# Gated delta attention and an expert layer: attention steps written out, zero-state products left out, balanced assignment on shares

## What is computed

```python
# attention, per head (8 heads, 128 x 128 state), token by token
Sst = Sst * a_t
kv = k_t @ Sst
delta = (v_t - kv) * b_t
Sst = Sst + outer(k_t, delta)          # Sst = 0 at the start of each sequence
o_t = q_t @ Sst * scale
# o -> rms_norm, gate, @ Wo; then x + h; then relu(m @ W_fc)^2 @ W_proj
# experts: assignment balanced by 20 Sinkhorn rounds on la = -logits / 0.05
for _ in range(20):
    la = la - logsumexp(la, axis=-1)   # over the 8 experts
    la = la - logsumexp(la, axis=-2)   # over the 4096 tokens
pi = exp(la)                           # top 2 of pi, y = W_down(silu(g) * u), weighted by pi
```

## Time and profile before

| | us |
|---|---|
| three runs, median (lowest to highest) | 2385.48 (2385.26 to 2387.36) |
| the profiled execution, its own time | 2388.1 |
| its span, first to last instruction | 2386.3 |
| TensorE matmul, busy | 2149.1 (90%) |
| VectorE, busy | 1797.3 (75%) |
| ScalarE, busy | 1076.0 (45%) |
| GpSimd, busy | 687.2 (29%) |
| chain that ended last | TensorE 70%, VectorE 18%, issue 5% |

### The profile page before, as it was taken

One profiled execution on the slowest core, in us unless ns is written; L12 is line 12 of the kernel. 1 busy time (PEld: TensorE's weight loads), 2 busy tenths in 40 slices (PEclk: granted clock), 3 DMA queues, 4 the chain that ended last, 5 costly groups with the idle time before them and its releaser, 6 DMA issues.

```text
span 2386.3 us, 50587 instructions
## 1 busy us (share of the span) xinstructions
PE 2149.1 (90%) x16283; PEld 1907.0 (80%) x16283; DVE 1797.3 (75%) x4328; ACT 1076.0 (45%) x2288; POOL 687.2 (29%) x1092
## 2 busy tenths in 40 slices
PE   4679999999999999999999998432799999999998
PEld 4568888888888888888888887322699999999887
DVE  6578888888888888888888885577667766676653
ACT  2334444444544445444454443222555555554542
POOL 0113232332323323233233332000343434344332
PEclk9989999999999999999999998755899999999999
DMA  5321212212122121221212211001344454455331
GB/s 193 105 36 37 56 36 50 42 37 56 36 50 42 37 56 36 49 42 36 57 36 47 43 35 23 11 0 55 136 159 154 170 179 151 159 164 172 115 128 18
DMA packets 307785, 181.73 MB, mean 76 GB/s; under 512 B 244716, under 2 KB 286064, under 8 KB 298512
## 3 DMA queue, kind: packets, MB, share of 16 engines
q1 hardware_dynamic: 255184, 149.21, 21.8%
q0 software_dynamic: 11280, 29.31, 4.3%
q10 hardware_dynamic: 41264, 2.51, 1.1%
HBM read 150.23 MB, written 32.51 MB: 77 GB/s over the span
## 4 chain that ended last, share of the span: by engine, by line
PE 70%; DVE 18%; issue 5%; DMA 2%; ACT 2%; SPq 2%; DVEq 0%; POOL 0%; ACTq 0%; POOLq 0%
PE ps_front L745 12%; PE ps_inva L745 9%; PE ps_invb L745 9%; PE ps_back L745 9%; PE ps_back L1939 7%; PE ps_back L2000 4%; PE ps_back L1983 4%; PE ps_back L2010 4%; DVE o_s L1679 3%; DVE r_s L1639 3%; PE ps_front L1883 2%; PE ps_invb L1933 1%; DVE aP L1567 1%; PE ps_inva L1922 1%; PE ps_back L1843 1%
## 5 line engine op out<-in xcount | busy, mean ns | idle before, releaser
L615 DVE TENSOR_TENSOR w_lo<-w_raw,w_hi 128x512 fp32r<-128x512 f32 x288 | 190.2, 688 | 4.0
L745 PE MATMUL ps_back<-w_hi,eh_hi 128*128 128x256 f32 x624 | 180.1, 289 | 3.2 <-DVE eh_lo L625 3.2
L745 PE MATMUL ps_back<-w_hi,eh_lo 128*128 128x256 f32 x624 | 176.5, 283 | 0.1
L745 PE MATMUL ps_back<-w_lo,eh_hi 128*128 128x256 f32 x624 | 176.4, 283 | 0.0
L699 ACT ACTIVATE w_hi<-w_raw 128x512 fp32r<-128x512 f32 x288 | 169.9, 627 | 0.0
L711 ACT ACTIVATE sact<-ps_inva 128x512 f32<-128x512 f32 (+1 forms) x96 | 49.8, 519 | 237.4 <-PE ps_inva L745 212.4
L1266 ACT ACTIVATE v_s<-ps_front 128x512 f32<-128x512 f32 x64 | 38.1, 595 | 234.5 <-PE ps_front L745 234.5
L1266 ACT ACTIVATE g_s<-ps_front 128x512 f32<-128x512 f32 x64 | 38.4, 599 | 228.3 <-PE ps_front L745 216.7
L745 PE MATMUL ps_inva<-xT_hi,w_hi 128*128 128x512 f32 (+1 forms) x384 | 135.5, 353 | 1.8 <-DVE xT_lo L620 1.7
L1883 PE MATMUL ps_front<-kqT_t 128*128 128x256 f32 x512 | 127.5, 392 | 9.1 <-DVE aP L1567 9.1
L745 PE MATMUL ps_inva<-xT_lo,w_hi 128*128 128x512 f32 (+1 forms) x384 | 135.0, 352 | 0.0
(11 more groups left out here) (373 smaller groups left out, 6672.5 us busy)
## 6 DMA issues: line engine op xcount, KB each, us to landing
w_raw<-L_ffn_W_gate_dram SPq DMA_DIRECT2D x24, 1024.0 KB
w_raw<-L_ffn_W_up_dram SPq DMA_DIRECT2D x24, 1024.0 KB
w_raw<-L_ffn_W_down_dram SPq DMA_DIRECT2D x24, 1024.0 KB
dT<-alphaT_d SPq DMA_DIRECT2D x32, 512.0 KB, 3.7
x_all<-L_attn_x_dram SPq DMA_DIRECT2D x4, 1024.0 KB, 9.4
hTr<-hT_d SPq DMA_DIRECT2D x32, 128.0 KB, 3.5
lt_d<-aP SPq DMA_DIRECT2D x256, 8.0 KB, 1.5
xi<-low_d SPq DMA_DIRECT2D x32, 128.0 KB
```

Source lines behind the costliest of these rows:

```text
L615: V.tensor_tensor(piece(w_lo[p], m).bitcast(F32R), piece(w_raw, m), piece(w_hi[p], m), ALU.subtract).then_inc(split[n], 1)
L745: ins = MM(out_, w[a].bitcast(F32R), x[b].bitcast(F32R), start=start and n == 0, stop=stop and n == 2)
```

## The change

The steps of the attention are written out on SP, ScalarE, VectorE and TensorE (TensorE still waits for its weights after step 0); GpSimd's loop stays. In the first chunk of a sequence (t % 4 == 0), where the state is zero, state_k, state_q and scaled_qs are left out; r becomes minus vb by one instruction of 128 x 1024 with a semaphore r_negated, on which ScalarE's silu of v and TensorE's state_u wait; state_o and state_out become copies out of PSUM. In the last chunk (t % 4 == 3) state_out is left out on TensorE and VectorE. The semaphore targets come from the written order. The assignment takes one Exp of la (times e^69), then 19 rounds on the shares themselves: reciprocal of the column sums, scaling, row sums, reciprocal, scaling, column sums, one TensorE product. All sums are kept, and their logarithms are subtracted from la half-way, where the shares are renewed by an Exp, and at the end.

```diff
+        def first_chunk(t):
+            return t % CHUNKS == 0
+        def last_chunk(t):
+            return t % CHUNKS == CHUNKS - 1
...
 # VectorE, assignment
+            dve.wait_ge(shares_made, 1)
+            ch.link(V.tensor_reduce(cols_, by_expert(shares), X, ALU.add))
...
+            def subtract_logs(first, last):
+                dve.wait_ge(rows_logged, 1 if last == HALF else 2)
+                ch.link(V.tensor_reduce(rows_, row_logs[:, first + (first == 0):last, :].rearrange("p n t -> p t n"), X, ALU.add))
+                ch.link(V.tensor_tensor(la[:, :, :], la[:, :, :], per_head(rows_, E), ALU.subtract))
+                dve.wait_ge(cols_logged, 1 if last == HALF else 2)
+                ch.link(V.tensor_reduce(colm, col_logs[:, first:last, :].rearrange("p n e -> p e n"), X, ALU.add))
+                ch.link(V.tensor_tensor(la[:, :, :], la[:, :, :], over_tiles(colm), ALU.subtract))
+            for n in range(1, ROUNDS):
+                if n == HALF:
+                    subtract_logs(0, HALF)
+                    dve.wait_ge(shares_made, 2)
                 else:
+                    dve.wait_ge(cols_summed, n)
+                    ch.link(V.reciprocal(col_inv, col_sums(n - 1)))
+                    ch.link(V.scalar_tensor_tensor(shares, over_tiles(col_inv), SPREAD, shares, ALU.mult, ALU.mult))
+                ch.link(V.tensor_reduce(row_sums[:, n, :], shares, X, ALU.add))
+                ch.link(V.reciprocal(row_inv, row_sums[:, n, :]))
+                ch.link(V.scalar_tensor_tensor(shares, per_head(row_inv, E), SPREAD, shares, ALU.mult, ALU.mult))
+                ch.link(V.tensor_reduce(cols_, by_expert(shares), X, ALU.add))
+            subtract_logs(HALF, ROUNDS)
...
 # TensorE, assignment
+            for n in range(ROUNDS):
+                pe.wait_ge(sk_dve, shares_at(n))
+                MM(col_sums(n), ones[:, :], cols_, start=True, stop=True).then_inc(cols_summed, 1)
...
 # VectorE, attention
+                if first_chunk(t):
+                    V.tensor_scalar(r_s[:, :], vb[:, :], -1.0, None, ALU.mult).then_inc(r_negated, 1)
+                    return
...
+                    if first_chunk(t):
+                        V.tensor_copy(o_s[:, s], psB[u % 2][:, :]).then_inc(back_evac[u % 2], 1)
+                        continue
...
             def state_out(t, p):
+                if last_chunk(t):
+                    return
...
+                    if first_chunk(t):
+                        V.tensor_copy(state[:, g * GW:(g + 1) * GW], psB[u % 2][:, :]).then_inc(back_evac[u % 2], 1)
+                        continue
...
-            step(0, 0, True, True, False)
-            with dve.Fori(0, PAIRS - 1) as i:
-                for p in range(2):
-                    step(2 * i + p + 1, 1 - p, True, True, True)
-            step(TILES - 3, 1, True, True, True)
-            step(TILES - 2, 0, True, False, True)
-            step(TILES - 1, 1, False, False, True)
+            for t in range(TILES):
+                step(t, t % 2, t + 1 < TILES, t + 2 < TILES, t > 0)
...
 # TensorE, attention
+                    if first_chunk(t):
+                        pe.wait_ge(r_negated, t // CHUNKS + 1)
...
-                state_k(t)
+                if not first_chunk(t):
+                    state_k(t)
...
-                    state_q(t, [g])
+                    if not first_chunk(t):
+                        state_q(t, [g])
...
-                state_out(t, p)
+                if not last_chunk(t):
+                    state_out(t, p)
```

More of the change, by code:

```diff
@@ L285, in f_evac, with back_uses @@
             return FU // 2 * f + u // 2 + 2
-        def b_filled(s, u):
[L292 to L296, removed]
+        def first_chunk(t):
+            return t % CHUNKS == 0
+        def last_chunk(t):
+            return t % CHUNKS == CHUNKS - 1
+        def back_uses(s):
+            skipped = set()
+            if s == 0:
+                skipped |= set(TAIL_USES)
+            if s == TILES:
+                skipped |= set(STATE_USES)
+            if first_chunk(s):
+                skipped |= {BU_KS, BU_KS + 1, BU_QS, BU_QS + 1}
+            if last_chunk(s):
+                skipped |= {BU_KDU, BU_KDU + 1}
+            return [(s, u) for u in range(BU) if u not in skipped]
+        back_order = [use for s in range(TILES + 1) for use in back_uses(s)]
+        back_counts = {}
+        for s, u in back_order:
+            back_counts[s, u] = 1 + sum(1 for other in back_counts if other[1] % 2 == u % 2)
+        def b_filled(s, u):
+            return back_counts[s, u]
         def b_evac(s, u):
@@ L670, in act_late, with logs @@
             act.preload_act_table_set("natural_log_exp_and_others")
[L671 to L684, removed]
+            act.wait_ge(sk_dve, 2)
+            A(se, sd, ACT.Exp).then_inc(sk_act, 1)
+            act.wait_ge(sk_dve, 4)
+            A(rowl, rows_, ACT.Ln).then_inc(sk_act, 1)
+            act.wait_ge(sk_dve, 7)
+            act.wait_ge(spread_ready, 1)
+            A(shares, la[:, :, :], ACT.Exp, bias=log_spread).then_inc(shares_made, 1)
+            def logs(first, last):
+                r = slice(first + (first == 0), last)
+                act.wait_ge(sk_dve, shares_at(last - 1) - 3)
+                A(row_logs[:, r, :], row_sums[:, r, :], ACT.Ln, scale=TOKENS / E / SPREAD).then_inc(rows_logged, 1)
+                act.wait_ge(cols_summed, last)
+                A(col_logs[:, first:last, :], psB[0][:, first * E:last * E].rearrange("p (n e) -> p n e", e=E), ACT.Ln, scale=E / TOKENS / SPREAD).then_inc(cols_logged, 1)
+            logs(0, HALF)
+            act.wait_ge(sk_dve, shares_at(HALF - 1) + SK_LOGS)
+            A(shares, la[:, :, :], ACT.Exp, bias=log_spread).then_inc(shares_made, 1)
+            logs(HALF, ROUNDS)
+            act.wait_ge(sk_dve, shares_at(ROUNDS - 1) + SK_LOGS)
             A(pi, la[:, :, :], ACT.Exp).then_inc(sk_act, 1)
-            act.wait_ge(sk_act, SK_A * (ROUNDS // GROUP) + 1)
+            act.wait_ge(sk_act, 3)
             with nc.allow_non_contiguous_dma(reason="weights beside each row"):
@@ L1090, in _ @@
             pairs_to_blocks(0)
-            step(0, 0, True, True, True, False)
-            with sp.Fori(0, PAIRS - 1) as i:
-                for p in range(2):
[L1094 to L1097, removed]
+            for t in range(TILES):
+                step(t, t % 2, t + 1 < TILES, t + 2 < TILES, t + 3 < TILES, t > 0)
             sp_late(sp)
@@ L1259, in silu @@
                 u = (FU_K, FU_Q, FU_V, FU_G)[n // 2] + n % 2
-                if not first and n == 4:
+                if not first and n == 4 and first_chunk(f - 1):
+                    act.wait_ge(r_negated, (f - 1) // CHUNKS + 1)
+                elif not first and n == 4:
                     for g in range(G):
@@ L2090, in _ @@
             pe.wait_ge(vg_split, 4 * KD + 1)
[L2091 to L2095, removed]
-            step(TILES - 2, 0, True, False, True)
-            step(TILES - 1, 1, False, False, True)
+            for t in range(1, TILES):
+                step(t, t % 2, t + 1 < TILES, t + 2 < TILES, True)
             tail_o(TILES - 1), tail_wo(TILES - 1)
```

90 lines of the change are left out of this document (40 added, 50 removed).

## The result

| | kernel before | changed kernel |
|---|---|---|
| median (lowest to highest), us | 2386.42 (2385.26 to 2389.69), 4 runs | 2366.72 (2360.51 to 2367.96), 4 runs |
| ratio | | 0.991, 95% interval 0.9898 to 0.9922 |
| profiled execution, its own time and span | 2388.1, 2386.3 | 2367.62, 2365.9 |
| mean granted clock | 0.957 | 0.954 |

What follows compares the result with a forecast made beforehand. TensorE was taken to bound the attention, a chain of small waiting instructions the balanced assignment. Terms -10.5 + 6.3 - 0.5 + 13 - 31.3 = -23 us gave 2362 us for the median, range 2346 to 2380.

Steps and rivals of the forecast that it cites:

- term 5: Attention steps 3 to 28 written out: code not run before costs 0.5 us per step, +13 us, bounds 4 and 28.
- term 2: TensorE's new idle time before block_t at seven inner boundaries lowers the clock: 0.9 us each, +6.3 us.
- term 1: State products left out at seven inner boundaries: the DMA then sets block_t, 1.5 us gained each, -10.5 us.
- term 6: Balanced assignment: rounds of 3.34 us instead of 5.05, 31.3 us less.
- terms 1 and 3: State products left out at the boundaries, -10.5 us, and VectorE's copies in step 0, about -0.5 us.
- first-chunk steps 1 to 2 us under the others: Sign in the attention's profile after that would show the forecast right: first-chunk steps shorter by 1 to 2 us.
- Step 0 and 31, evacuations: Step 0 about -0.5 us by VectorE's copies; step 31 nothing; ScalarE's and VectorE's evacuations and the r_negated wait nothing.
- rival (a): Attention: written-out steps cost nothing lasting, 0.17 us per step, +4 instead of +13 us, 2353 us; chance 0.28.
- Rival (c): Attention: SP queue becomes the bound, steps cost 2.2 us more, 57 instead of 13, slower at 2406 us; chance 0.06.
- Rival (d): Assignment isn't shorter: reciprocals take 1.75 us at any width, rounds 6.3 us, 56 us more, 2418 us; chance 0.02.

Runs made afterwards that it cites:

- the fill: Changed kernel with 22 identity transposes on TensorE ahead of block_t at the seven inner boundaries: 2353.1 us, ratio 0.9855.
- the repeat run: The changed kernel once more, unaltered, on the chip of the kernels compared with it: 2365.75 us, ratio 0.9906 to the kernel before.
- nothing left out: Changed kernel with zero-state products and last updates computed again, steps written out, new assignment; two runs: 2361.24 us (0.9889) and 2360.8 us (0.9895).
- the assignment alone: Kernel before with only the new assignment on shares, attention and loops as before; two runs: 2354.78 us (0.9866) and 2355.52 us (0.9874).
- the inverse first: Changed kernel with VectorE's pair_inverse ahead of tail_xf in last chunks: 2353.08 us, ratio 0.9863.

## Why the prediction was right, point by point

The sum was -23 us and -20 came. That it comes so close is partly luck: term 5 was 8 us too dear and term 2 some 6 us too cheap, and these two errors nearly cancel. The two large readings, the DMA chain in term 1 and the assignment in term 6, hold.

1. **State products, -10.5 us: right.** The DMA of x4 sets block_t: the step into a boundary is about 1.2 us shorter with the fill (41.5 on average against 42.76) and 0.75 and 0.92 in the two profiles without it, instead of 5.85. GpSimd's last root instruction starts 7.4 us after the last L2046 (1158.20 - 1150.78 in the repeat run), forecast with 7.1, since VectorE's product now falls on GpSimd's chain so that one instruction of it takes 1.38 us, where in the earlier trace rows's step one took 0.99. With the clock kept (the fill), leaving out is worth 8 to 10 us against nothing left out; terms 1 and 3 said 11. That is a difference of ratios from different chips.
2. **The clock, +6.3 us: right in kind, half the size.** The fill gives back 12.6. I priced 16 products at half clock (at most 1.5 us); the low stretch covers some 6 us of work, and a step after a boundary took up to 3.9 us more than with the fill (46.17 against 42.28 at t = 24). Five of seven boundaries paid in the first profile (block_t at 483.97 and 998.99 kept 1.00), seven of seven in the second. By the Trainium skill's rule ("TensorE: Matmul & The Clock Gate", section "HAM oscillation — how this bites in real kernels") each boundary pays, and the traces nearly agree, with 12 of 14. The sign "first-chunk steps 1 to 2 us under the others" came only in part: the steps into a boundary were 0.75 and 0.92 us under, those after it 1.2 and 1.7 over, in the two profiles.
3. **Step 0 and 31, evacuations:** no gain is seen. Step 0 took 41.9 and 41.8 us instead of 40.2, but also 42.3 where only SyncE was written out and nothing left out, so half a microsecond can't be read from it. There is no wait for r_negated among TensorE's waits.
4. **Steps written out, +13 us: mis-sized, and its mechanism wrong.** It measured +5.2 (2.9 to 7.9 by the interval), near rival (a)'s +4. The step that failed was to read the earlier trace rows as "SyncE in new code" and to carry a mean of three steps, all next to the entry or exit of the loops, over 26 others. With SyncE alone in new code the bursts don't stretch away from the others' loop ends, and with all four written out five of the seven long bursts lie in steps of 42.8 us. The waits for hid_lo hardly grow by writing out alone (2.9 us against 2.7; 6.2 and 3.8 in the two profiles of the changed kernel), and most steps cost under 0.1 us (42.8 against 42.76). Rival (c) falls by the same rows: no step is over 44.03 us.
5. **Assignment, -31.3 us: right.** 30.4 in the trace, 30 and 32 in the runs; reciprocals 0.21 and 0.35 us, forecast 0.21 and 0.36. Rival (d) falls.

So +5 (written out), +4 (left out, with its clock loss) and -31 make -22. The best versions have no loss of clock: the assignment with the fill (0.9855) and the assignment alone (0.9866 and 0.9874) aren't told apart by these intervals, nor is the inverse first (0.9863); all beat the changed kernel.

## What to carry to other kernels

Before leaving out work of the busiest engine, look for what else its next instruction waits for: here a DMA chain with 0.6 us of slack took most of 5.85 us, and the idle time that came in its place cost more in clock than was won. If such a gap can't be closed, fill it with harmless products, or start the chain behind it earlier, and measure each part of a change by itself: a gain of 31 us hid a loss of 9. Writing 28 steps out cost 5 us in all, a loop of two steps nothing, and a loop of four steps 21 us: try the body's length before choosing it, since a body that is too long pays at every return.

## What was not expected of the hardware

- A body of four steps costs TensorE about 3 us of issue at each return and mostly half clock after it, +21 us in all; a body of two steps costs nothing that the trace shows.
- A GpSimd instruction of one column takes 1.35 instead of 0.27 us beside VectorE's 128x1024 product of two SBUF inputs.
- SyncE's bursts of DMA issues stretch (3.62 to some 5 us) where the other engines enter or leave their loops, and in some steps where all run new code, but not where only SyncE does.
- 22 transposes that compute nothing, in a wait of 2.4 to 3.1 us at seven boundaries, make the kernel 12.6 us faster.
- The clock falls after some waits and not after others of the same length: with waits of 2.83 and 2.79 us it stayed at 1.00, with 2.62 and 1.67 it fell.
